# GpSimd drains after every group of four indirect DMAs in a graph network kernel

## The chip, the cores and the metric

The kernel runs on one core of one Trainium2 chip. The metric is the device time of one execution in microseconds (us), lower is better. Before the change it is 5252.78 us, the median of 3 runs (5245.05 to 5259.6).

## The reference

The program is a pre-norm graph network on 100,000 nodes with 128 features and 25,000 edges (src, dst). It adds four layers to x, one after the other, each on `h = relu(layernorm(x))`:

```python
x = x + gcn(h)      # sum over edges of w * h[dst] into src, plus h/degree
x = x + sage2(h)    # two SAGE convolutions: mean over edges of h[src] into dst, two matmuls each
x = x + mlp(h)      # message MLP on [h[src], h[dst], edge_attr], mean into dst, update MLP, layernorm
x = x + mean(h)     # mean over edges of h[dst] into src, two matmuls, relu
```

Each layer reads rows of nodes by the edges' indices and sums messages by the edges' other end. Nodes with no edge need only the parts without neighbours ("dense" work).

## The kernel before

All edges are padded to 50 chunks of 512 (P = 128 partitions, T = 4 tiles), worked on as 10 rounds (RD) of 5 streams (G); chunk `i * G + c` is round i of stream c. Six stages follow the setup: gcn, sage1, sage2, mlp, mean and final. Each stage is one block of five engine programs, and ends with a drain and a barrier on every engine (the block's end, and lines 854 and 855). The first five also carry the dense work of all 100,000 rows as further streams, whose steps stand in the same queues on TensorE, VectorE, ScalarE and SyncE.

GpSimd (POOL) issues only indirect DMAs in the stages, one for each tile of 128 edges, so four for a chunk and purpose:
- **Gathers** (`gather`, L567, recorded as L569): a row of a table in HBM for each of 128 indices, into one tile of SBUF. Each stage has a local `pair(n, i, c)` that issues two of them (L1241 gcn, L1394 sage1, L1542 sage2, L1727 mlp, L1985 mean, L2134 final). A chunk has pairs 0 and 1, in gcn and mlp also 2 and 3 from a second table. A pair is a step `fetch0`, `fetch1`, and so on; `fetch0` of the next round waits until the chunk's buffer has been read by another engine.
- **Adds** (`add_pair`, L1139, recorded as L1151): rows of SBUF are added to a table in HBM by the DMA engines. Since two adds to one row must not overlap, the plan makes one chain over all streams: `add_pair` waits until the pair before in the chain has landed (the `wait_ge` on `e.added`). gcn, sage1 and mlp have steps `add0` and `add1` of two DMAs; sage2 and mean have one step `add` of four.
- **Row writes** (`write_chunk`, L2057, recorded as L2061): in final, four indirect DMAs write a chunk's rows to the output, once for the dst side (`write_d`) and once for the src side (`write_s`). These have a chain as well.

The setup issues 200 gathers of its own (`gathered`, L569 with the tile `xs`), directly and not by `pair`.

The order of the steps on each engine is fixed when the program is built: `Plan` (L278 on) makes a list schedule of all streams' steps with a length for each (FETCH 2600 ns a pair, ADD 3800 ns a pair of adds, 5100 for a row write, LANDED 2800 ns from an add to the next of the chain) and with due times of a table; `rounds` replays this order on every engine. The lengths steer the order only. On the chip each step waits for semaphores: `e.done[c]` counts a stream's steps, `e.gathered[c]` and `e.added[c]` its landed DMAs.

On GpSimd a stage is therefore: the first gathers of all five streams, then the steps in the plan's order, and at its end waits for all adds or writes:

```python
def step(name, i, c):
    if name == "fetch0" and not is_last(i):
        pool.wait_ge(e.done[c], at.after(i, "x1"))
    if name.startswith("fetch") and not is_last(i):
        pair(int(name[5:]), i + 1, c)
    if name in ("add", "add0", "add1"):
        add_pair(pool, e, plan, tb.node, k.leadh, name, i, c, W1)
```

Chunks of a round are consumed a round later than they are fetched: the gathers of round i + 1 are issued in round i, and `keep` (L1176, ScalarE) may overwrite the rows of the adds of round i only when they have landed.

Of the kernel before, what the change touches and what calls it, by code (L numbers as in the profile page):

```python
# [12 lines left out]
T = 4  # L13
# [327 lines left out]
def rounds(step, plan):  # L341

    for name, i, s in plan.order:
        step(name, i, s)
# [32 lines left out]
def is_last(i):  # L377
    return i == RD - 1
# [183 lines left out]
def fill_nodes(steps):  # L562

    return [Node(f"fill{q}", SYNC, 100, after=((step, 0, 0),), main=False) for q, step in enumerate(steps)]

def gather(pool, out, table, idx, signal, offset=0):  # L567

    pool.indirect_dma_start(out, None, table, bass.IndirectOffsetOnAxis(ap=idx, axis=0),  # L569
                            element_offset=offset).then_inc(signal, 16)  # L570
# [568 lines left out]
def add_pair(pool, e, plan, table, leads, name, i, c, offset):  # L1139

    parts = {"add0": range(U), "add1": range(U, T), "add": range(T)}[name]
    pool.wait_ge(e.done[c], e.at.after(i, "keep"))
    held = plan.prior.get((c, name, i))
    if held is not None:
        prior, pair, j = held
        pool.wait_ge(e.added[prior], (j * T + (U if pair == "add0" else T)) * 16)
    for t in parts:  # L1150
        pool.indirect_dma_start(table, bass.IndirectOffsetOnAxis(ap=leads[:, i * G + c, t:t + 1], axis=0), e.comb[c][:, t, :], None,  # L1151
                                element_offset=offset, compute_op=ALU.add).then_inc(e.added[c], 16)

def edge_tail(columns, sum_on, match_after=(), bank=None, whole=False):
# [23 lines left out]
def gcn_phase(nc, k, tb, inp, out):  # L1179

    with ExitStack() as ctx:
# [53 lines left out]
        @block.gpsimd  # L1236
        def _(pool):
            for c in L:
                nc.gpsimd.memset(e.comb[c][:, :, :], 0.0).then_inc(blank, 1)

            def pair(n, i, c):  # L1241
                for t in (2 * n % T, 2 * n % T + 1):
                    at_dst = k.gidx[:, i * G + c, T + t:T + t + 1]
                    if n < 2:
                        gather(pool, x[c][:, t, :], inp["x"], at_dst, e.gathered[c])
                    else:
                        gather(pool, sm[c][:, t, :], tb.small, at_dst, e.gathered[c])

            def step(name, i, c):
                if c >= G:  # L1250
                    return
                if name == "fetch0" and not is_last(i):
                    pool.wait_ge(e.done[c], at.after(i, "y"))
# [3 lines that stand above are left out]
                    add_pair(pool, e, plan, tb.node, k.leads, name, i, c, 0)  # L1257

            for c in L:
                for n in range(4):  # L1260
                    pair(n, 0, c)
            rounds(step, plan)
            for c in L:
                pool.wait_ge(e.added[c], RD * T * 16)
# [59 lines left out]
def sage1_phase(nc, k, tb, inp, out):  # L1324
# [3 lines left out]
    with ExitStack() as ctx:  # L1328
# [63 lines left out]
        @block.gpsimd  # L1392
        def _(pool):
            def pair(n, i, c):  # L1394
                for t in (2 * n, 2 * n + 1):
                    gather(pool, agg[c][:, t, :], tb.node, k.gidx[:, i * G + c, t:t + 1], e.gathered[c])

            def step(name, i, c):
                if c >= G:
                    return  # L1400
# [7 lines that stand above are left out]
            for c in L:  # L1408
                for n in range(2):
                    pair(n, 0, c)  # L1410
            rounds(step, plan)
            for c in L:
                pool.wait_ge(e.added[c], RD * T * 16)
# [70 lines left out]
def sage2_phase(nc, k, tb, inp, out):  # L1484

    with ExitStack() as ctx:
# [52 lines left out]
        @block.gpsimd  # L1540
        def _(pool):
            def pair(n, i, c):  # L1542
                for t in (2 * n, 2 * n + 1):
                    gather(pool, a[c][:, t, :], tb.node, k.gidx[:, i * G + c, t:t + 1], e.gathered[c], W1)

            def step(name, i, c):
                if c >= G:
                    return
                if name == "fetch0" and not is_last(i):
                    pool.wait_ge(e.done[c], at.after(i, "mix"))  # L1550
# [3 lines that stand above are left out]
                    add_pair(pool, e, plan, tb.node, k.leadd, name, i, c, W2)  # L1554

            for c in L:
                for n in range(2):
                    pair(n, 0, c)
            rounds(step, plan)
            for c in L:  # L1560
                pool.wait_ge(e.added[c], RD * T * 16)
# [60 lines left out]
def mlp_phase(nc, k, tb, inp, out):  # L1622
# [3 lines left out]
    with ExitStack() as ctx:  # L1626
# [98 lines left out]
        @block.gpsimd  # L1725
        def _(pool):
            def pair(n, i, c):  # L1727
                for t in (2 * n % T, 2 * n % T + 1):
                    if n < 2:
                        gather(pool, a2[c][:, t, :], tb.node, k.gidx[:, i * G + c, t:t + 1], e.gathered[c], W2)  # L1730
                    else:
                        gather(pool, w[c][:, t, :], tb.node, k.gidx[:, i * G + c, T + t:T + t + 1], gathered2[c])

            def step(name, i, c):
                if c >= G:
                    return
                if name == "fetch0" and not is_last(i):
                    pool.wait_ge(e.done[c], at.after(i, "plus_d"))
# [3 lines that stand above are left out]
                    add_pair(pool, e, plan, tb.sums, k.leadh, name, i, c, 0)  # L1742

            for c in L:
                for n in range(4):
                    pair(n, 0, c)
            rounds(step, plan)
            for c in L:
                pool.wait_ge(e.added[c], RD * T * 16)
# [174 lines left out]
def mean_phase(nc, k, tb, inp, out):  # L1924
# [3 lines left out]
    with ExitStack() as ctx:  # L1928
# [54 lines left out]
        @block.gpsimd  # L1983
        def _(pool):
            def pair(n, i, c):  # L1985
                for t in (2 * n, 2 * n + 1):
                    gather(pool, s3[c][:, t, :], tb.sums, k.gidx[:, i * G + c, T + t:T + t + 1], e.gathered[c])

            def step(name, i, c):
                if c >= G:  # L1990
                    return
                if name == "fetch0" and not is_last(i):
                    pool.wait_ge(e.done[c], at.after(i, "mix_u"))
# [3 lines that stand above are left out]
                    add_pair(pool, e, plan, tb.sums, k.leads, name, i, c, D)  # L1997

            for c in L:
                for n in range(2):  # L2000
                    pair(n, 0, c)
            rounds(step, plan)
            for c in L:
                pool.wait_ge(e.added[c], RD * T * 16)
# [52 lines left out]
def write_chunk(pool, table, rows, idx, signal):  # L2057

    for t in range(T):  # L2060
        pool.indirect_dma_start(table, bass.IndirectOffsetOnAxis(ap=idx[:, t:t + 1], axis=0), rows[:, t, :], None,  # L2061
                                bounds_check=N - 1, oob_is_err=False).then_inc(signal, 16)

class FinalSide:
# [11 lines left out]
def final_phase(nc, k, tb, out):  # L2077
# [4 lines left out]
    with ExitStack() as ctx:  # L2082
# [50 lines left out]
        def _(pool):  # L2133
            def pair(n, i, c):  # L2134
                for t in (2 * n, 2 * n + 1):
                    gather(pool, s34[c][i % 2][:, t, :], tb.sums, k.gidx[:, i * G + c, t:t + 1], e.gathered[c][i % 2])

            def write(name, rows, idx, i, c):
                held = plan.prior.get((c, name, i))
                if held is not None:  # L2140
                    prior, _, j = held
                    pool.wait_ge(written[name][prior], (j + 1) * T * 16)
                write_chunk(pool, out, rows, idx, written[name][c])
# [13 lines left out]
            for c in L:  # L2157
                for n in range(2):
                    pair(n, 0, c)
# [99 lines left out]
```

## Time and profile before

| | |
|---|---|
| Time of the runs | 5252.78 us, median of 3 |
| The profiled execution, first to last instruction | 6243.6 us |
| Mean granted TensorE clock | 0.836 |
| Busy: PE, PEld | 68%, 53% |
| Busy: DVE, ACT | 66%, 59% |
| Busy: POOL | 61% |
| Indirect DMAs issued by POOL | 3200: 200 in the setup, 3000 in the stages |
| DMA engines: hardware queues, POOL's queue | 32.9% and 22.7% of 16 engines |
| Chain that ended last, traced part | mostly "another core or an unknown queue" (6%) in the last stage |

The profiled execution is one execution with the hardware profiler on. Its span is 990.8 us longer than the median of the runs; the page gives no time of it other than the span.
### The profile page before, as it was taken

The numbers are of one execution on the slowest core, as the hardware profiler recorded it, in microseconds if no ns is written. First come the engines' busy times: TensorE is split into PE (matmuls) and PEld (weight loads), VectorE is DVE, ScalarE is ACT, GpSimd is POOL, SyncE is SP. The second block draws the span as 40 slices with busy tenths as digits, with TensorE's granted clock in tenths as the row PEclk, the third lists the DMA queues.
The fourth block names the chain that finished last, engine by engine and source line by source line (L and its number), as shares of the span: only waits on it lengthen the run. The fifth ranks groups of instructions, "written<-read, shape, count | busy, mean of one in ns | idle before, by whom it ended". The sixth has DMA issues, their size and how long they took to land. (4 is left out here: it accounts for less than half of the span.)

```text
span 6243.6 us, 88780 instructions
## 1 busy us (share of the span) xinstructions
PE 4227.3 (68%) x25124; PEld 3337.9 (53%) x25124; DVE 4147.6 (66%) x20553; ACT 3656.1 (59%) x9152; POOL 3838.7 (61%) x3228
## 2 busy tenths in 40 slices
PE   1173777777566766998958888886888846545444
PEld 1052555556455555777736666664666634434333
DVE  1094777778699995776747777785999945434334
ACT  0003767767577774776746677774877845434333
POOL 6605666675577765776747677765777654544554
PEclk7596888888788887999979999998999967667666
DMA  9903656666466664666658788884555531211221
GB/s 251 311 2 112 181 154 172 167 166 169 115 153 151 148 144 113 146 144 132 130 147 220 209 225 216 225 204 113 136 132 128 122 77 58 76 53 63 66 65 36
DMA packets 891523, 878.84 MB, mean 141 GB/s; under 512 B 131106, under 2 KB 671660, under 8 KB 890962
## 3 DMA queue, kind: packets, MB, share of 16 engines
q1 hardware_dynamic: 546568, 575.48, 29.0%
q0 software_dynamic: 224000, 235.91, 22.7%
q10 hardware_dynamic: 120460, 61.78, 3.7%
q8 instruction: 198, 3.24, 0.2%
q14 instruction: 297, 2.43, 0.1%
HBM read 345.70 MB, written 533.16 MB: 141 GB/s over the span
## 5 line engine op out<-in xcount | busy, mean ns | idle before, releaser
L2061 POOL DMA_INDIRECT out<-final_y,leads x200 | 202.2, 1011 | 434.8 <-DVE final_y L2188 328.8
L1151 POOL DMA_INDIRECT node<-gcn_comb,leads x200 | 325.2, 1626 | 193.0 <-ACT gcn_comb L1176 92.5
L1151 POOL DMA_INDIRECT sums<-mean_comb,leads x200 | 327.6, 1638 | 154.1 <-ACT mean_comb L1176 84.4
L1151 POOL DMA_INDIRECT node<-sage_comb,leadh x200 | 329.4, 1647 | 142.4 <-DMA node<-sage_comb,leadh 60.8
L444 PE MATMUL final_p<-wT,final_hT 128*128 128x128 f32 x800 | 223.0, 393 | 274.9 <-remote 141.4
L1151 POOL DMA_INDIRECT sums<-mlp_same,leadh x200 | 325.7, 1628 | 131.4 <-issue 54.2
L1151 POOL DMA_INDIRECT node<-sage_comb,leadd x200 | 319.5, 1597 | 140.7 <-issue 54.2
L839 PE MATMUL hist<-lo,hi 128*126 128x400 f16 x800 | 162.1, 361 | 261.4 <-issue 136.3
L444 PEld LDWEIGHTS final_p<-wT,final_hT 128*128 128x128 f32 x800 | 170.8, 264 | 305.1 <-remote 144.9
L569 POOL DMA_INDIRECT mlp_a<-node,gidx x200 | 207.2, 1036 | 197.2 <-DVE mlp_v L1778 128.6
L785 DVE TENSOR_SCALAR hi<-iota,parts 128x252 f16<-128x252 f16 x400 | 146.0, 378 | 245.7 <-remote 159.0
L569 POOL DMA_INDIRECT gcn_x<-in_x,gidx x200 | 198.1, 991 | 168.8 <-DVE gcn_y L1283 107.1
L444 PE MATMUL gcn_p<-wT,gcn_dhT 128*128 128x128 f32 x1056 | 228.9, 346 | 76.6 <-ACT gcn_dhT L986 40.0
L839 PEld LDWEIGHTS hist<-lo,hi 128*126 128x126 f16 x800 | 114.2, 148 | 309.6 <-DVE lo L786 140.8
L569 POOL DMA_INDIRECT sage_agg<-node,gidx x200 | 203.6, 1018 | 110.4 <-issue 49.4
L437 PE MATMUL final_p<-ident,final_h 128*128 128x128 f32 x600 | 120.3, 339 | 213.5 <-ACT final_h L431 141.7
L444 PEld LDWEIGHTS gcn_p<-wT,gcn_dhT 128*128 128x128 f32 x1056 | 194.0, 228 | 117.3 <-ACT gcn_dhT L986 50.2
L569 POOL DMA_INDIRECT mean_s<-sums,gidx x200 | 202.5, 1013 | 83.7 <-issue 57.3
L437 PE MATMUL sage_p<-ident,sage_dh 128*128 128x128 f32 x840 | 150.0, 310 | 151.4 <-ACT sage_dh L431 109.3
L569 POOL DMA_INDIRECT sage_a<-node,gidx x200 | 200.3, 1001 | 80.8 <-issue 57.5
L569 POOL DMA_INDIRECT xs<-in_x,gidx x200 | 194.8, 974 | 86.9 <-issue 62.2
L431 ACT ACTIVATE sage_dh<-sage_dx,sage_dn_shift,sage_dn_rstd 128x128 f32<-128x128 f32 x560 | 228.5, 482 | 32.8 <-DVE sage_dn_shift L420 14.9
(367 smaller groups left out, 17207.2 us busy)
## 6 DMA issues: line engine op xcount, KB each, us to landing
node<-b SPq DMA_DIRECT2D x400, 256.0 KB
sums<-zero_row SPq DMA_DIRECT2D x400, 256.0 KB
node<-zero_row ACTq DMA_DIRECT2D x50, 1152.0 KB
sage_dx<-in_x SPq DMA_DIRECT2D x70, 256.0 KB
out<-sage_dy SPq DMA_DIRECT2D x70, 256.0 KB
gcn_dx<-in_x SPq DMA_DIRECT2D x66, 256.0 KB
out<-gcn_dy SPq DMA_DIRECT2D x66, 256.0 KB
x_src<-xs SPq DMA_DIRECT2D x50, 256.0 KB
```

What stands on the lines that cost most here:

```text
L431: tiles(lambda t: nc.scalar.activation(out[:, t, :], x[:, t, :], func, bias=b.sh[:, t:t + 1], scale=b.rs[:, t:t + 1])).then_inc(done, 1)
L437: return tiles(lambda t: nc.tensor.transpose(ps[:, t * P:(t + 1) * P], x[:, t, :], ident))
L444: last = nc.tensor.matmul(o, xT[:, t * P:(t + 1) * P], w, start=True, stop=plus is None and bias is None)
L569: pool.indirect_dma_start(out, None, table, bass.IndirectOffsetOnAxis(ap=idx, axis=0), element_offset=offset).then_inc(signal, 16)
L785: nc.vector.tensor_scalar(hi[c][:, n * T + t, :], iota[:, 0:2 * HIGH], part[:, 0:1], None, ALU.is_equal)
L839: last = nc.tensor.matmul(hist[0:HIGH, n, b, 0:LOW], hi[c][:, n * T + t, b * HIGH:(b + 1) * HIGH], lo[c][:, n * T + t, :], start=False, st ...
L1151: pool.indirect_dma_start(table, bass.IndirectOffsetOnAxis(ap=leads[:, i * G + c, t:t + 1], axis=0), e.comb[c][:, t, :], None, element_off ...
L2061: pool.indirect_dma_start(table, bass.IndirectOffsetOnAxis(ap=idx[:, t:t + 1], axis=0), rows[:, t, :], None, bounds_check=N - 1, oob_is_er ...
```

## The change

A new function `settle` issues one drain on GpSimd. It is called behind the fourth gather of each group of four (pair 1, and in gcn and mlp also pair 3), behind the fourth add of a chunk, and behind the fourth row write of a chunk. The setup's gathers are left as they are. The plan and its lengths are not changed, and neither is any wait.

```diff
+def settle(pool):
+
+    pool.drain()
+
+
 def gather(pool, out, table, idx, signal, offset=0):
...
     for t in parts:
         pool.indirect_dma_start(table, bass.IndirectOffsetOnAxis(ap=leads[:, i * G + c, t:t + 1], axis=0), e.comb[c][:, t, :], None,
                                 element_offset=offset, compute_op=ALU.add).then_inc(e.added[c], 16)
+        if t == T - 1:
+            settle(pool)
...
                     else:
                         gather(pool, sm[c][:, t, :], tb.small, at_dst, e.gathered[c])
+                if n % 2 == 1:
+                    settle(pool)
...
             def pair(n, i, c):
                 for t in (2 * n, 2 * n + 1):
                     gather(pool, agg[c][:, t, :], tb.node, k.gidx[:, i * G + c, t:t + 1], e.gathered[c])
+                if n % 2 == 1:
+                    settle(pool)
...
     for t in range(T):
         pool.indirect_dma_start(table, bass.IndirectOffsetOnAxis(ap=idx[:, t:t + 1], axis=0), rows[:, t, :], None,
                                 bounds_check=N - 1, oob_is_err=False).then_inc(signal, 16)
+        if t == T - 1:
+            settle(pool)
```

The `pair` functions of sage2, mlp, mean and final get the same two lines as that of sage1.

## Rows read from the trace of the kernel before

**Rows 1.** Windows by stage: us; busy us (count) of PE, PEld, DVE, ACT, POOL.
```profile
476.00:1645.00 1169.00, 818.72 (x4960) 646.12 (x4960) 839.37 (x4522) 784.34 (x2000) 725.86 (x605) 0.83 0.59 156
1645.00:2430.00 785.00, 499.23 (x2800) 388.17 (x2800) 691.28 (x3850) 556.15 (x1450) 532.97 (x400) 0.83 0.61 140
2430.00:3172.00 742.00, 640.63 (x4280) 543.19 (x4280) 503.62 (x2190) 503.45 (x1200) 519.71 (x400) 0.95 0.62 135
3172.00:4296.00 1124.00, 916.59 (x5510) 701.97 (x5510) 793.37 (x3630) 754.12 (x1850) 734.25 (x600) 0.91 0.77 203
4296.00:5068.00 772.00, 617.53 (x3660) 489.93 (x3660) 659.50 (x3180) 579.48 (x1450) 530.15 (x400) 0.92 0.54 123
5068.00:6244.00 1176.00, 569.41 (x3100) 452.00 (x3100) 469.76 (x2350) 476.36 (x1200) 592.59 (x600) 0.69 0.21 63
```

**Rows 2.** Waits of POOL for other engines: us in total, times, longest; and one issue gap.
```profile
POOL out L2061 <- DVE final_y L2188: 328.8, 27, 35.3
...
POOL mlp_a L569 <- DVE mlp_v L1778: 128.6, 22, 32.3
...
POOL gcn_x L569 <- DVE gcn_y L1283: 107.1, 14, 14.7
POOL node L1151 <- ACT gcn_comb L1176: 92.5, 11, 18.1
POOL sums L1151 <- ACT mean_comb L1176: 84.4, 14, 12.0
POOL node L1151 <- ACT sage_comb L1176: 75.9, 18, 9.2
...
POOL gcn_sm L569 <- issue: 60.6, 199, 0.3
...
POOL sage_agg L569 <- DVE sage_x L1434: 49.2, 33, 6.3
```

**Rows 3.** The same view: waits of POOL for an add's landing.
```profile
POOL node L1151 <- DMA node<-sage_comb,leadh: 60.8, 28, 4.1
...
POOL sums L1151 <- DMA sums<-mlp_same,leadh: 44.3, 15, 4.3
...
POOL node L1151 <- DMA node<-gcn_comb,leads: 37.7, 13, 4.1
...
POOL node L1151 <- DMA node<-sage_comb,leadd: 23.3, 8, 3.9
...
POOL sums L1151 <- DMA sums<-mean_comb,leads: 10.7, 4, 3.3
```

**Rows 4.** Timeline of POOL in sage1: start us, us, what, idle time before.
```profile
2311.43 2.07 POOL L1151 DMA_INDIRECT node<-sage_comb,leadh  x1 [0.31 <-issue]
2315.99 1.73 POOL L1151 DMA_INDIRECT node<-sage_comb,leadh  x1 [2.49 <-DMA node<-sage_comb,leadh]
```

**Rows 5.** Drains on POOL by line: ns min/median/max, first and last start us.
```profile
L576 POOLq DRAIN  x1: 26153/26153/26153, 280.6 to 280.6; - x1
...
L1182 POOLq DRAIN  x1: 6830/6830/6830, 1637.2 to 1637.2; - x1
...
L2082 POOLq DRAIN  x1: 9032/9032/9032, 6233.7 to 6233.7; - x1
...
L854 POOLq DRAIN  x6: 107/119/157, 1644.3 to 6242.9; - x6
...
L855 POOLq DRAIN  x6: 46/46/46, 1644.8 to 6243.3; - x6
```

**Rows 6.** Timeline of POOL: the last indirect DMAs of the setup, gcn and final.
```profile
289.62 1.09 POOL L569 DMA_INDIRECT xs<-in_x,gidx  x1 [0.30 <-issue]
...
1633.65 1.54 POOL L1151 DMA_INDIRECT node<-gcn_comb,leads  x1 [0.30 <-issue]
...
6231.33 0.97 POOL L2061 DMA_INDIRECT out<-final_y,leads  x1 [0.30 <-issue]
```

**Rows 7.** Busy tenths of the DMA engines, 290 to 310 us in 40 slices.
```profile
DMA  9999814999659925999999999620000000000000
```

More of the change, by code:

```diff
@@ L1544, in pair @@
                     gather(pool, a[c][:, t, :], tb.node, k.gidx[:, i * G + c, t:t + 1], e.gathered[c], W1)
+                if n % 2 == 1:
+                    settle(pool)
             def step(name, i, c):
@@ L1732, in pair @@
                         gather(pool, w[c][:, t, :], tb.node, k.gidx[:, i * G + c, T + t:T + t + 1], gathered2[c])
+                if n % 2 == 1:
+                    settle(pool)
             def step(name, i, c):
@@ L1987, in pair @@
                     gather(pool, s3[c][:, t, :], tb.sums, k.gidx[:, i * G + c, T + t:T + t + 1], e.gathered[c])
+                if n % 2 == 1:
+                    settle(pool)
             def step(name, i, c):
@@ L2062, in write_chunk @@
                                 bounds_check=N - 1, oob_is_err=False).then_inc(signal, 16)
+        if t == T - 1:
+            settle(pool)
 class FinalSide:
@@ L2136, in pair @@
                     gather(pool, s34[c][i % 2][:, t, :], tb.sums, k.gidx[:, i * G + c, t:t + 1], e.gathered[c][i % 2])
+                if n % 2 == 1:
+                    settle(pool)
             def write(name, rows, idx, i, c):
```

## The prediction

> **What bounds the kernel now.** I read the windows by stage first, because a mean over the span hides stages with different limits. In none of the six stages is an engine busy throughout [rows 1]: POOL has 726 of 1169 us in gcn, 533 of 785 in sage1, 520 of 742 in sage2, 734 of 1124 in mlp, 530 of 772 in mean, 593 of 1176 in final. But busy time is not all that POOL's queue costs. Next come the waits of POOL: each indirect DMA starts 0.30 us after the end of the one before even where nothing holds it (60.6 us over 199) [rows 2]. With 600, 400, 400, 600, 400 and 600 DMAs that is 180 or 120 us a stage. POOL's own work is then 906, 653, 640, 914, 650 and 773 us, which is 78, 83, 86, 81, 84 and 66% of the stages. So in the first five stages POOL is as near to a bound as the busiest other engine (DVE 88% in sage1, PE 86% in sage2 and 82% in mlp), and in final it waits for others.
>
> What POOL waits for otherwise is short. The six largest of its waits for VectorE and ScalarE in the first five stages come to 538 us (128.6 + 107.1 + 92.5 + 84.4 + 75.9 + 49.2), and final's largest to 329 us [rows 2]. Its waits for an add to land are few, 68 over 400 steps of adds, 177 us in all [rows 3]. The reason is in the plan: a pair of gathers usually stands between two pairs of adds, so that the landing passes behind other descriptor work. That cover is what the change touches.
>
> **What a drain waits for.** The change removes nothing and moves nothing. It adds 750 drains: 150 in gcn (two groups of gathers and one of adds for each of 50 chunks), 100 in sage1, 100 in sage2, 150 in mlp, 100 in mean, 150 in final (one of gathers, two of row writes). No stage of the kernel before has a drain within its work, but each has some at its end, and the setup has one directly behind its gathers. That one began at 280.6 us, while gathers were still queued in front of it, and lasted 26.15 us, to 306.8 us [rows 5]. The last gather ended on POOL at 290.7 us [rows 6], and the DMA engines went quiet in the 27th half-microsecond after 290, at about 303.5 us [rows 7]. So this drain did not end with the descriptors, but after the data. I take it that a drain on POOL ends only when all indirect DMAs before it have landed.
>
> The Trainium skill (Perfetto Trace Analysis, Per-engine timelines) puts DRAIN under the instructions that the sequencer handles alone, with no other actor than the semaphores. By that rule 750 drains would cost what L855's do, 46 ns each, some 35 us; the 26.15 us drain disagrees with it.
>
> **Price of one drain.** It has three terms.
> First, the landing and the restart. They have rows where an add waits for the pair before: idle 2.49 us in place of 0.30 [rows 4], and on average 37.7/13 = 2.90 us in gcn, 60.8/28 = 2.17 in sage1, 23.3/8 = 2.91 in sage2, 44.3/15 = 2.95 in mlp, 10.7/4 = 2.68 in mean [rows 3]. I use them for gathers too, whose landing has no row of its own. From each goes the 0.30 us gap that was there anyway. For final's row writes the nearest row is its end: the last write ended at 6232.3 us [rows 6] and the drain behind its landing wait began at 6233.7 [rows 5], 1.4 us. The restart adds 0.5: in gcn the same stretch was 2.0 us (1635.2 to 1637.2), where a wait up to the next add is 2.50.
> Second, the drain's own time once all has landed. The ends are far apart: 0.05 to 0.16 us for a drain shortly after another, and 6.8 and 9.0 us for the ones at the ends of gcn and final, which began when everything had landed already [rows 5]. In between lies what has been issued since the last drain: nothing in the one case, some 600 DMAs in the other. Per DMA that is 6.83/600 = 0.011 us; the setup's drain gives at most (306.8 - 290.7)/200 = 0.08. Four DMAs are far nearer to none than to 200, so I take 0.12 plus a share for four, between 0.17 and 0.44: 0.26 us.
> Third, what is queued behind. Every later gather and add of all streams is held, and the pair of gathers that used to hide the landing of an add cannot do so across a drain. The other engines wait for these DMAs a round later, so a single drain harms nobody; the sum on POOL does.
> That makes 2.86, 2.13, 2.87, 2.91, 2.64 and (1.4 + 0.5 - 0.3 + 0.26) 1.86 us a drain.
>
> **The sum**, stage by stage, is POOL's work plus its drains against the stage's present length:
> gcn 906 + 150 x 2.86 = 1335, 166 over 1169. sage1 653 + 213 = 866, 81 over. sage2 640 + 287 = 927, 185 over. mlp 914 + 437 = 1351, 227 over. mean 650 + 264 = 914, 142 over. Together 801 us, if POOL never waited for another engine. It will: at a stage's start and end, and where the fixed order is unlucky. I keep 30% of the 538 us, 161 us; the rest is slack that drains fill. In final 773 + 279 = 1052 us is still below 1176, so it isn't bound by POOL; but its chains go through POOL's queue, and I let half of the 279 us show, 140 us. The setup is unchanged. Sum: 801 + 161 + 140 = 1102 us on a span of 6243.6 us, 17.7%.
> The median of the runs, 5252.8 us, is 990.8 us below that span. Scaled with it, the new time is 6180 us; if the landing, which isn't the engines' work, keeps its length, it is 5253 + 1102 = 6355. I take the middle, **6270 us**.
> The bounds: with no slack filled at all, all drains show, 1630 + 279 = 1909 us, which is 6860 to 7160 us. With all slack filled and drains of 2.0 us in place of 2.7, 801 falls to some 370 us to which a part of the slack is added: about 5700 us.
>
> **Rivals.**
> The fixed price. The 6.8 to 9.0 us of the late drains are paid by each drain that has any DMA before it. For it: the setup's (200 DMAs) and gcn's and final's (600) are not in proportion to their number. Against it: a second drain costs 0.12 us. Then POOL would carry 4536 us of stage work plus 750 x 9 us, 11,300 us, and the time is 9500 to 12,000 us. Chance 0.07.
> The cheap drain. It waits only until the descriptors are made, and costs 0.12 us and a cold restart, 0.2 to 0.4 us in all, 150 to 300 us on POOL, a good third of them visible: 5300 to 5400 us. For it: the short drains of L854 and L855. Against: the setup's. This is near what the skill's rule above says. Chance 0.05.
> The other side, not slower. The drain is the sequencer's alone, which reads ahead: the setup's began 9 us before the last gather did. If it holds only the sequencer, for 46 ns, then it is over before the queued DMAs are and POOL sees no gap; 35 us spread over 750 places vanish, also if the builder drops drains as empty. It decides for a drain that ends before the last DMA in front of it does. The time would be 5253 us. The only such drain of the trace ended 16 us after it. Chance 0.04, with 0.01 of it for a gain by DMAs that collide less.
> The forecast has 0.84.
>
> **Chances and range.** 0.3%, 16 us, is about what a measurement of this kernel can tell from no change. The range reaches from 5700 to 7100 us: the forecast's two bounds. It leaves out the rivals, 0.16. Faster 0.01, same 0.03, slower 0.96.
>
> **What the profile after would show.** 750 more DRAIN rows on POOL at `settle`'s line, with a median of 2 to 4 us each, as they start while DMAs before them still run. Idle time of POOL before the first DMA of each group of 2 to 3 us instead of 0.30. The 2.5 us waits for adds should mostly vanish, as a drain has taken them over. POOL's waits for VectorE and ScalarE should shrink in the first five stages, and waits of VectorE and TensorE for DMAs should grow. The drains at the stages' ends should fall from 6 to 9 us to well below 1 us; if they don't, the second term is wrong. All stages should be longer, mlp by most. I am wrong if drains have a median under 0.5 us, or over 6 us, or if the stages grow by the full 1909 us, which would mean that slack fills nothing.

## The result and the profile after

The changed kernel takes 7015.3 us, the median of 4 runs (7009.0 to 7029.18), against 5250.07 us for the kernel before (4 runs, 5245.05 to 5259.6). The ratio is 1.3357, interval 1.3327 to 1.3387: slower by 1765 us. The forecast was 6270 us. The direction and the range held; the size was too small by 745 us.

The page of the changed kernel begins:

```profile
span 7027.4 us, 89530 instructions
PE 4295.2 (61%) x25124; PEld 3406.3 (48%) x25124; DVE 4128.4 (59%) x20553; ACT 3649.4 (52%) x9152; POOL 3866.6 (55%) x3228
```

The span agrees with the runs here. For the profile of before it did not (6243.6 against 5253 us), so the first experiment took a new profile of the unedited kernel, on a chip where it runs in 5265 us (`ctrl`, below). Its page begins:

```profile
span 5246.6 us, 88780 instructions
PE 4000.3 (76%) x25124; PEld 3169.2 (60%) x25124; DVE 4131.0 (79%) x20553; ACT 3632.5 (69%) x9152; POOL 3860.8 (74%) x3228
```

It is the code of [rows 1] with the same count of instructions and, within 2%, the same busy time of DVE, ACT and POOL, in a span 997 us shorter. Against this profile the change has to be read. The windows by stage of the changed kernel (us; busy us of PE, PEld, DVE, ACT, POOL; clock, DMA share, GB/s):

```profile
338.00:1669.00 1331.00, 820.03 (x4960) 654.58 (x4960) 829.25 (x4520) 783.02 (x2000) 730.07 (x605) 0.81 0.51 137
1669.00:2631.00 962.00, 544.12 (x2800) 426.33 (x2800) 689.53 (x3850) 555.25 (x1450) 531.04 (x400) 0.74 0.50 114
2631.00:3546.00 915.00, 654.20 (x4280) 558.89 (x4280) 501.58 (x2190) 502.24 (x1200) 515.21 (x400) 0.85 0.50 110
3546.00:4973.00 1427.00, 910.54 (x5510) 702.32 (x5510) 786.23 (x3630) 746.63 (x1850) 721.40 (x600) 0.81 0.61 160
4973.00:5908.00 935.00, 656.66 (x3660) 517.20 (x3660) 658.83 (x3180) 579.52 (x1450) 529.49 (x400) 0.84 0.44 102
5908.00:7027.00 1119.00, 558.85 (x3100) 438.86 (x3100) 467.40 (x2350) 480.61 (x1200) 596.06 (x600) 0.70 0.22 66
```

and of the unedited kernel in `ctrl`:

```profile
321.00:1300.00 979.00, 752.87 (x4960) 597.08 (x4960) 828.78 (x4520) 777.94 (x2000) 734.25 (x605) 0.90 0.69 186
1300.00:2056.00 756.00, 488.39 (x2800) 380.26 (x2800) 688.86 (x3850) 554.88 (x1450) 535.62 (x400) 0.85 0.64 145
2056.00:2745.00 689.00, 622.32 (x4280) 530.32 (x4280) 500.83 (x2190) 500.26 (x1200) 519.93 (x400) 0.97 0.66 146
2745.00:3736.00 991.00, 883.22 (x5510) 678.91 (x5510) 787.18 (x3630) 743.87 (x1850) 727.90 (x600) 0.95 0.85 230
3736.00:4450.00 714.00, 595.73 (x3660) 472.09 (x3660) 655.53 (x3180) 578.28 (x1450) 533.94 (x400) 0.95 0.58 133
4450.00:5247.00 797.00, 506.38 (x3100) 402.08 (x3100) 469.22 (x2350) 475.12 (x1200) 600.35 (x600) 0.80 0.31 93
```

No engine does more in its stage than before, except that TensorE's matmuls are longer where its clock is lower (0.79 of full speed over the run): it idles between chunks. All six stages grew: by 352, 207, 225, 436, 222 and 323 us, together 1764 before rounding. The setup adds 17 us (338 in place of 321); `gathers` and `spaced` below have the same 17 us, `adds` and `twice` do not, and the setup has none of the new drains, so it isn't they, and it stays unexplained.

In `ctrl`, DMA instructions, memsets and the 0.30 us between them fill POOL for 914, 656, 640, 908, 654 and 780 us, 4552 of the 4925 us of the stages, 92%; in final 98%. That is the prediction's "POOL's own work", as it had it (906, 653, 640, 914, 650, 773), in stages that are 4 to 32% shorter than those of [rows 1].

Now the drains. By line, on POOL (ns min/median/max, first and last start), with those at the ends of gcn and final, which were 6.8 and 9.0 us [rows 5]. The source lines of this kernel are some lines further on than before (L1151 is now L1156, for example):

```profile
L569 POOLq DRAIN  x750: 3405/5973/13829, 340.1 to 7021.4; - x188
...
L1189 POOLq DRAIN  x1: 147/147/147, 1668.1 to 1668.1; - x1
...
L2101 POOLq DRAIN  x1: 53/53/53, 7026.5 to 7026.5; - x1
```

A row of 6 us doesn't mean that a drain costs 6 us: it starts when the sequencer reaches it, with DMAs of the group still before it on the engine. What it costs is seen from POOL's timeline, here in sage1 (start, us, what, idle before):

```profile
2104.02 1.02 POOL L574 DMA_INDIRECT sage_agg<-node,gidx  x1 [0.30 <-issue]
2105.35 0.98 POOL L574 DMA_INDIRECT sage_agg<-node,gidx  x1 [0.31 <-issue]
2108.97 1.62 POOL L1156 DMA_INDIRECT node<-sage_comb,leadh  x1 [2.65 <-issue]
2110.90 1.68 POOL L1156 DMA_INDIRECT node<-sage_comb,leadh  x1 [0.30 <-issue]
...
2115.67 1.02 POOL L574 DMA_INDIRECT sage_agg<-node,gidx  x1 [3.10 <-issue]
```

Behind the fourth gather POOL is idle 2.65 us, behind the fourth add 3.10 us, where the gap would otherwise be 0.30. The trace also has the time at which the DMA engines moved the last packet of each group. With it, the mean over the drains splits into 1.70 us from the last DMA's end on POOL to the landing (0.85 to 0.97 for row writes, 3.3 for mlp's gathers from `node`), 0.57 us from the landing to the drain's end, and 0.78 us to the next DMA: 3.05 in place of 0.30 us, so **2.75 us a drain**. The shortest time from the landing to a drain's end is 0.39 us, and no packet of POOL's queue lands between the end of a drain and the next DMA. 750 of them are 2063 us in POOL's queue. 4552 + 2063 = 6615 us, and the stages take 6689. POOL's queue is now all but the whole time.

POOL's waits agree (us in total, times, longest). "Issue" now holds most of the drains. The wait for `final_y` that was the largest of before [rows 2] is gone. The waits for adds to land [rows 3] seem to be all still there:

```profile
POOL node L1156 <- issue: 409.4, 513, 5.8
POOL sums L1156 <- issue: 307.3, 345, 7.9
POOL out L2078 <- issue: 297.0, 383, 5.0
POOL mlp_w L574 <- issue: 248.7, 200, 6.4
...
POOL node L1156 <- DMA node<-sage_comb,leadh: 55.5, 19, 4.0
POOL node L1156 <- DMA node<-gcn_comb,leads: 53.1, 18, 3.5
POOL node L1156 <- DMA node<-sage_comb,leadd: 41.4, 13, 4.5
POOL sums L1156 <- DMA sums<-mlp_same,leadh: 34.7, 13, 3.6
...
POOL sums L1156 <- DMA sums<-mean_comb,leads: 19.3, 7, 3.0
```

That is 204 us in 70 waits, against 213 in 87 in `ctrl`. But the timeline has a drain in 41 of the 70: there the view puts the drain's time down to the landing, which comes shortly before the drain's end. Only 29, 81 us, are waits at which no drain stood. They are all in gcn, sage1 and mlp, where a chunk's adds are two pairs and no drain stands between them, and 28 of them come directly behind another add. In sage2 and mean, where the four adds are one step, none is left. Waits of POOL over 0.5 us without a drain come to 102 us in 37 places in all.

### The profile page after: what moved, and what is told of

It reads as the page before. It is cut to its first block and busy times, and to the rows that moved or that the text cites. A ratio compares the mean times of both kernels' runs of the same rounds, so it can differ in the third digit from the quotient of the medians.

```text
span 7027.4 us, 89530 instructions
## 1 busy us (share of the span) xinstructions
PE 4295.2 (61%) x25124; PEld 3406.3 (48%) x25124; DVE 4128.4 (59%) x20553; ACT 3649.4 (52%) x9152; POOL 3866.6 (55%) x3228
## 5 line engine op out<-in xcount | busy, mean ns | idle before, releaser
L1156 POOL DMA_INDIRECT sums<-mlp_same,leadh x200 | 324.6, 1623 | 272.2 <-issue 149.9
L1156 POOL DMA_INDIRECT node<-sage_comb,leadh x200 | 327.5, 1638 | 236.9 <-issue 131.3
L1156 POOL DMA_INDIRECT node<-gcn_comb,leads x200 | 322.5, 1612 | 226.1 <-issue 143.3
L1156 POOL DMA_INDIRECT sums<-mean_comb,leads x200 | 325.6, 1628 | 205.4 <-issue 157.3
L1156 POOL DMA_INDIRECT node<-sage_comb,leadd x200 | 317.1, 1586 | 191.0 <-issue 134.7
L476 PE MATMUL mlp_p<-mlp_same,mlp_v 128*128 128x256 f32 x400 | 122.7, 460 | 390.8 <-DVE mlp_same L1089 390.7
L574 POOL DMA_INDIRECT mlp_w<-node,gidx x200 | 197.2, 986 | 248.7 <-issue 248.7
L1089 DVE TENSOR_SCALAR mlp_same<-mlp_krow,rec 128x256 f32<-128x256 f32 x200 | 69.8, 412 | 405.2 <-DMA sums<-mlp_same,leadh 404.1
L574 POOL DMA_INDIRECT gcn_sm<-small,gidx x200 | 198.8, 994 | 196.4 <-issue 196.4
L437 PE MATMUL gcn_p<-ident,gcn_dh 128*128 128x128 f32 x792 | 140.7, 309 | 264.9 <-ACT gcn_dh L431 264.3
L574 POOL DMA_INDIRECT final_s<-sums,gidx x200 | 198.0, 990 | 183.4 <-issue 169.8
L431 ACT ACTIVATE mlp_dh<-mlp_dx,mlp_dn_shift,mlp_dn_rstd 128x128 f32<-128x128 f32 x240 | 98.5, 483 | 381.1 <-DVE mlp_dn_shift L420 380.4
L476 PEld LDWEIGHTS mlp_p<-mlp_same,mlp_v 128*128 128x128 f32 x400 | 87.3, 230 | 411.3 <-DVE mlp_same L1089 396.9
L2078 POOL DMA_INDIRECT out<-final_od,final_rows_d x200 | 199.1, 995 | 158.3 <-issue 147.5
L574 POOL DMA_INDIRECT xs<-in_x,gidx x200 | 234.8, 1174 | 85.7 <-issue 60.7
```

What stands on the lines that cost most here:

```text
L431: tiles(lambda t: nc.scalar.activation(out[:, t, :], x[:, t, :], func, bias=b.sh[:, t:t + 1], scale=b.rs[:, t:t + 1])).then_inc(done, 1)
L437: return tiles(lambda t: nc.tensor.transpose(ps[:, t * P:(t + 1) * P], x[:, t, :], ident))
L476: last = nc.tensor.matmul(ps[:, h * HALF:(h + 1) * HALF], msg[:, b, :], same[:, block, :], start=(n == 0), stop=(n == len(terms) - 1))
L1089: last = nc.vector.tensor_scalar(e.same[c][:, t, :], key_half(e, c, t), field(k, i, c, key)[:, t:t + 1], weight[:, t:t + 1], ALU.is_equal, ...
```

## The experiments

None of them leaves out or changes a part of the computation. Ratios are to the kernel before on the same chip. The question was where the missing 745 us were: in the price of a drain (theory A: each is dearer than 2.55 us), or in the slack (theory B: the price is nearly right, but far less of it is hidden). The rival to both was that the drain isn't a wait for landing at all but a fixed cost.

### On a chip where the kernel before takes 5265 us

**ctrl**: the kernel before, unedited.

> The kernel before, not edited. The profile of before spans 6243.6 us where its runs took 5250; the profile of the changed kernel spans 7027 where its runs took 7015. Theory: that one profiled execution of before was held up by the recording (its setup ended at 486 us with VectorE stalls of 40 us, that of the changed kernel some 150 us sooner), and a second profile of the same kernel spans 5250 us within 1%. Rival: the profiler always adds some 990 us to this kernel, and the second profile spans 6200 us or more; then the 1765 us of the runs and the 784 us between the two profiles disagree for a reason that lies in the change.

Measured 5247.41 us, ratio 0.9984 (0.996 to 1.0008), and the profile above. Its span is 997 us below that of the profile the prediction read, for the same code. So a profile doesn't add the 991 us. Nor was it a recording that held up one execution, as was expected: on three other chips (below) the kernel before takes 6103 to 6226 us, the medians of 8 to 19 runs. The difference is a property of the chip or of its state. The lower clock of TensorE (0.836 in place of 0.901) doesn't explain it: TensorE is busy 227 us more in the first profile, not 997.

**gathers**: drains behind gathers only, 400 of them.

```diff
-        if t == T - 1:
-            settle(pool)
```

(in `add_pair` and in `write_chunk`)

> Drains behind the groups of gathers alone, 400 of 750. Theory (every drain holds GpSimd's queue until the four DMAs before it have landed, 2.75 us more than the 0.30 us gap, and what slack the stages have is filled first): 400 x 2.8 = 1120 us on the queue, 250 of it hidden in slack, 6050 to 6200 us. Rival (the drains behind adds carry the cost, since these hold the chain of adds, and gathers are fetched a round ahead and can land whenever they like): under 5600 us.

Measured 6362.19 us, 1.2112 (1.1991 to 1.2233): +1097 us over the 5264.83 of before, or 2.74 us a drain. More than expected.

**adds**: the other 350, behind adds and row writes.

```diff
-                if n % 2 == 1:
-                    settle(pool)
```

(in all six `pair` functions)

> Drains behind adds and row writes alone, 350 of 750. Theory (queue time is queue time): 250 x 2.7 + 150 x 2.1, with the group of adds often followed by a wait for their landing anyway: 5750 to 6000 us, and the two halves together show less than the whole, as each fills the same slack. Rival (the chain of adds carries the cost): 6500 us or more, nearly the whole loss.

Measured 6003.44 us, 1.1429 (1.1341 to 1.1517): +739 us, 2.11 us a drain, just above the expected band (whose sum counts 150 row-write drains where there are 100). Added up the two halves cost 1836 us, together 1765. If each alone had hidden much in slack that both share, the whole would cost more than the two added, as was expected; it doesn't, so hardly any slack of that kind was left on this chip, which speaks for B. A reason for costing less may lie in the line found by `spaced` below: all 3000 DMAs pay their 0.042 us once in either run alone, 126 us, and also only once together. But the intervals of the two runs, some 60 and 45 us either way, are as large as the difference of 71 us, so this isn't shown.

**waits**: no drain, and in each place a wait for the semaphore of the same four DMAs, as in sage1:

```diff
-                    settle(pool)
+                    pool.wait_ge(e.gathered[c], (i + 1) * T * 16)
```

> No drain; in each drain's place GpSimd waits for the semaphore of the same four DMAs. Theory (a drain is a wait for the landing, plus its own 0.57 us from the last completion packet to its end): a semaphore wait ends some 0.3 us after the packet and the next DMA starts 0.7 us later, so each group saves 0.2 to 0.3 us against the drain; 6780 to 6900 us. Rival (the cost is the drain's own, a flush of the engine and of the queue of instructions read ahead): under 5700 us.

Measured 6662.77 us, 1.2684 (1.2578 to 1.2791), 1398 us over its before and 352 us less than the drains, 0.47 us each. Below the expected band: more of the cost is the drain's own than was expected, but four fifths of it is there with no drain at all, as plain waiting for data. The timeline shows the same picture as with drains, with the landing now named as the releaser:

```profile
1800.77 0.98 POOL L569 DMA_INDIRECT sage_agg<-node,gidx  x1 [0.30 <-issue]
1803.61 1.62 POOL L1151 DMA_INDIRECT node<-sage_comb,leadh  x1 [1.85 <-DMA sage_agg<-node,gidx]
1805.53 1.75 POOL L1151 DMA_INDIRECT node<-sage_comb,leadh  x1 [0.30 <-issue]
1809.74 1.03 POOL L569 DMA_INDIRECT sage_agg<-node,gidx  x1 [2.47 <-DMA node<-sage_comb,leadh]
```

1.85 and 2.47 us in place of the 2.65 and 3.10 of the drains: 0.8 and 0.6 us less. That the drain waits for the landing is thereby shown, not only read from the setup's row.

**twice**: a drain for each pair, 1500 in all.

```diff
-                if n % 2 == 1:
-                    settle(pool)
+                settle(pool)
...
-        if t == T - 1:
+        if t in (U - 1, T - 1):
```

> A drain after every pair of gathers or of adds and after two of four row writes, 1500 drains. Theory (each drain holds the queue for a landing): the 750 further ones cost 2.5 to 2.75 us each, less where a wait for an add stood at that place anyway (some 150 of them), 1500 to 2000 us more, 8500 to 9000 us. Rival (the cost goes by the DMAs that must be cleared, so half as many a drain cost half): near 7015 us.

Measured 8676.2 us, 1.6492 (1.6417 to 1.6568): 1661 us over the changed kernel for 750 more drains, 2.2 us each, a little under the first 750's 2.35. This is what a landing costs again and again; a fixed 7 to 9 us would have added over 5000.

**spaced**: a drain only for every 2nd, 4th, 8th, 16th, 25th or 50th group, by stage, 128 in all.

```diff
+EVERY = {"gcn": 2, "sage1": 4, "sage2": 8, "mlp": 16, "mean": 25, "final": 50}
+STAGE = ["gcn", 0]
+
 def settle(pool):
-    pool.drain()
+    STAGE[1] += 1
+    if STAGE[1] % EVERY[STAGE[0]] == 0:
+        pool.drain()
```

(and each stage's function sets `STAGE` to its name and 0)

> Drains at growing distances: after every 2nd group of four DMAs in gcn, 4th in sage1, 8th in sage2, 16th in mlp, 25th in mean, 50th in final, 128 in all. It measures a drain's own time, from the last landing to its end, against the number of DMAs since the last drain, which was 0.57 us for 4 and 5.7 to 9.0 us for 400 to 600. Theory (the drain goes through a list of DMAs not yet cleared, which has a bound, at 0.03 to 0.08 us each): 0.8 us after 8, 1.0 after 16, 1.9 after 32, 3.5 after 64, and the 6 us reached at 100 to 200. Rival A (a fixed cost that falls due once enough DMAs have passed): a step from 0.6 to 6 us. Rival B (0.01 us for each DMA, no bound): 0.7 after 16, 1.0 after 64, 2.5 after 200. Whole time: 5250 plus 128 x 2.5 = 320 us and the rising own time, 5450 to 5650 us.

Measured 5603.88 us, 1.0649 (1.0605 to 1.0693): 343 us for 128 drains, 2.68 each. The run was for the drain's own time, which the prediction could not place between 4 and 200 DMAs. POOL's timeline has the idle time behind drains that close 8, 32, 64, 100 and 200 DMAs (gcn, sage2, mlp, mean, final; the rows of mlp and final close 66 and 202):

```profile
354.13 0.94 POOL L580 DMA_INDIRECT gcn_x<-in_x,gidx  x1 [3.11 <-issue]
...
2363.06 0.94 POOL L580 DMA_INDIRECT sage_a<-node,gidx  x1 [3.67 <-DVE sage_hT L1595]
...
3258.96 0.94 POOL L580 DMA_INDIRECT mlp_w<-node,gidx  x1 [6.16 <-issue]
...
4404.97 1.62 POOL L1162 DMA_INDIRECT sums<-mean_comb,leads  x1 [7.22 <-DVE mean_n_rstd L417]
...
5062.89 1.01 POOL L2089 DMA_INDIRECT out<-final_y,leads  x1 [9.47 <-issue]
```

The medians over the drains of a stage are 3.05 (8 DMAs), 3.29 (16), 4.15 (32), 6.38 (64), 7.2 (100) and 9.6 us (200). The part from landing to the drain's end, worked out from the packets of this run, of `twice`, `gathers`, `adds` and of the changed kernel, is 0.46 us with 2 DMAs since the last drain, 0.55 with 4, 0.71 with 8, 0.88 with 12, 1.04 with 16, 1.70 with 32, 3.15 with 64, 4.9 with 100. That is a line of about 0.38 + 0.042 us per DMA, close to the theory (0.8 after 8, 1.0 after 16, 1.9 after 32, 3.5 after 64). There is no step, as rival A had it, and the slope is four times rival B's. Up to 16 DMAs the same count gives the same time in runs that have it in different stages, so the stage isn't what counts. It doesn't go on: 198 to 202 DMAs give 4.5 us in the setup and 7.1 to 8.2 in final, both in this run, and the rows of the drains behind 400 to 600 are 5.7 to 9.0 us long.

The line is that of a drain that stands directly behind its DMAs and has begun before they land. A drain that begins only when all have landed costs twice as much for each. The ends of the stages in `gathers` and `spaced` show it, where POOL waits for all adds and then drains; these four rows close 16 DMAs (`spaced`) and 20, 38 and 40 (`gathers`):

```profile
L1507 POOLq DRAIN  x1: 1351/1351/1351, 3043.4 to 3043.4; - x1
...
L1496 POOLq DRAIN  x1: 1677/1677/1677, 3276.7 to 3276.7; - x1
...
L1187 POOLq DRAIN  x1: 3150/3150/3150, 1561.1 to 1561.1; - x1
...
L1941 POOLq DRAIN  x1: 3311/3311/3311, 5434.6 to 5434.6; - x1
```

They lie on 0.04 + 0.082 us per DMA, as do the ends with 28, 30 and 34. So a drain takes something for each DMA issued since the last drain, even when all of them have long landed. That a drain which begins early does half of this while it waits would explain the 0.042; it wasn't tested. At 0.082 us each, the 5.7 to 9.0 us behind 400 to 600 DMAs are worth some 70 to 110 DMAs (an estimate), so the bound lies about there.

### On chips where the kernel before takes 6100 to 6230 us

The next runs fell on other chips, on which the unedited kernel takes 6102.87, 6102.8 and 6226.07 us: the condition of the profile of before. Expectations in absolute times were mostly written for 5250; where the kernel before takes 6100 they can't be met, and the ratios and differences have to be compared.

**empty**: in each drain's place a wait that is always fulfilled.

```diff
-            settle(pool)
+            pool.wait_ge(e.done[c], 1)
```

> In each drain's place GpSimd waits for a count of 1 of the stream's own step semaphore, which is always reached already. The step costs the sequencer an instruction and the engine nothing. Theory (the landing is what costs): within 0.5% of the kernel before, 5230 to 5280 us. Rival (any instruction between two groups breaks the reading ahead, so that the next DMA starts 0.75 us after in place of 0.30): 750 x 0.45 = 340 us, 5500 to 5600 us.

Measured 6121.15 us, 1.0025 (1.001 to 1.004), 18 us. A wait for what is already reached costs next to nothing here. It is a weaker test than was meant: the 750 waits make only 239 further instructions (89019 in place of 88780), since the others are carried by an instruction that was there anyway, a DMA for example. The rival's price of 0.45 us for each would be 108 us for those 239. The 18 us speak against it, though on this chip part of what POOL's queue loses is hidden.

**empty2**: the same kernel again, on a third chip.

> The waits for what is always reached, once more. On the chip where the kernel before takes 6103 us they cost 0.25%, with GpSimd far from its bound. Where the kernel before takes 5250 us GpSimd's queue has 92% of the stages, and a step that broke the reading ahead would show in full. There: theory within 0.5%, 5230 to 5290 us; rival (0.45 us each) 5500 to 5600 us. If the job runs where before takes 6100: 1.0025 again, and the point stays open.

Measured 6260.05 us, 1.0073 (1.0039 to 1.0106), 34 us for 750 places, 0.05 us each, or 0.14 for each further instruction. The ratio is above the 1.0025 that was expected again. The cost where the kernel before takes 5250 us wasn't measured.

**double**: two drains in a row.

```diff
     pool.drain()
+    pool.drain()
```

> Two drains in a row in each place, 1500 in all, 750 of them with nothing to clear. Theory (a drain costs the landing of what is out, a fixed part of some 0.38 us and 0.04 us for each DMA cleared, and a second one finds nothing): 0.05 to 0.15 us each with the step between them, 40 to 150 us more than the changed kernel, 7050 to 7160 us. Rival (each drain has a fixed cost of 0.4 us or empties the engine anew for 0.75 us): 7300 to 7600 us.

Measured 7251.6 us, 1.1879 (1.1832 to 1.1926). Against `after2` below, from another chip with the same time of before, the second drains cost 104 us, 0.14 each. That is within the expected 40 to 150 us. Their rows say that a drain with nothing to wait for is nearly free:

```profile
L569 POOLq DRAIN  x750: 3659/5957/13092, 490.6 to 7258.0; - x188
...
L570 POOLq DRAIN  x750: 41/41/203, 498.0 to 7262.7; - x188
```

**finalonly** and **finalonly2** (one kernel, two chips): drains in the last stage alone, 150 of them.

```diff
-                if n % 2 == 1:
-                    settle(pool)
```

(in the other five `pair` functions, and the two lines in `add_pair`)

> Drains in the last stage alone, 150 of 750. In the prediction half of final's drain time was to be hidden, since POOL seemed 66% taken there; in the clean profile of the kernel before it is 98% taken (782 of 797 us). Theory now: nothing is hidden, the stage grows by 320 to 340 us as in the changed kernel, 5570 to 5600 us, and the other stages keep their length. Rival (the prediction's): 140 us, 5390 us.

> Drains in the last stage alone once more. On the chip where the kernel before takes 6103 us they cost nothing (0.996), its last stage being 1157 us long there with 774 of GpSimd's work. If this job runs where the kernel before takes 5250 and final 797 us: theory 5570 to 5600 us, nothing hidden; rival 5390 us, half of it hidden. If it runs where before takes 6100: 0.995 to 1.0 times before again.

Measured 6078.7 us, 0.9958 (0.9938 to 0.9978), and 6079.13 us, 0.9955 (0.9937 to 0.9973). On such chips the last stage takes 1125 and 1122 us with 150 drains, and 1157 to 1176 without a drain (the profile of before, `empty` and `empty2`); on the others 797 without and 1119 with. The drains fit entirely into time that POOL spent waiting, and on the slow chips the stage is even 32 us shorter than in `empty` on the same chip. What became of that waiting is told at the end of this section.

**after2**: the changed kernel.

> The changed kernel, not edited. The kernel before took 5250 to 5265 us in the first measurements and 6103 us on another chip, where VectorE got a count of TensorE in the setup some 40 us late. If this job runs where the kernel before takes 6100: theory (drains fill what time GpSimd has left, and there it has 850 us more to give) 7050 to 7150 us, 1.16 to 1.17 times before, in place of 1.336. Rival (the cost of a drain adds up whatever else waits): 6103 + 1765 = 7870 us. If it runs where the kernel before takes 5250: 7015 us again.

Measured 7147.89 us, 1.1715 (1.1692 to 1.1739), +1045 us, as the theory had it. Its windows of gcn and final:

```profile
486.00:1812.00 1326.00, 827.34 (x4960) 659.52 (x4960) 830.09 (x4520) 783.25 (x2000) 729.95 (x605) 0.80 0.51 137
...
6026.00:7148.00 1122.00, 565.40 (x3100) 443.57 (x3100) 468.42 (x2350) 480.06 (x1200) 596.84 (x600) 0.70 0.22 66
```

Beside the changed kernel's on the first chip (1331 and 1119) little differs but the setup, 486 in place of 338 us. The kernel before is 838 to 853 us slower on such a chip, the changed one 133 us. What makes these chips slow therefore costs almost nothing in the stages once the drains are there.

Where the time goes can be seen in the waits of the first profile. The largest are for "remote", a count on a semaphore that arrives with no instruction of the trace ending just before it (us in total, times, longest):

```profile
ACT final_hT L1899 <- remote: 217.9, 22, 25.2
DVE hi L785 <- remote: 159.0, 5, 41.8
PEld final_p L444 <- remote: 144.9, 13, 25.0
PE final_p L444 <- remote: 141.4, 13, 24.8
```

All of its "remote" waits come to 1902 us in 421 cases, on all engines together (where PE and PEld, or two engines behind one another, wait at the same time, it is counted twice); 939 us of them are in final. `ctrl` has none. `after2` has 173 us in 44 cases, and the largest three are in the setup:

```profile
DVE hi L790 <- remote: 111.9, 3, 41.8
```

The setup shows one of them closely. TensorE finished a row of 16 matmuls of L839 and then had nothing to do; in the first profile (PE, then DVE):

```profile
66.36 5.45 PE L839 MATMUL hist<-lo,hi 128*126 128x400 f16 x16 [10.02 <-issue]
107.44 2.93 PE L839 MATMUL hist<-lo,hi 128*126 128x400 f16 x8 [35.63 <-DVE lo L786]
```

```profile
103.87 0.29 DVE L785 TENSOR_SCALAR hi<-iota,parts 128x252 f16<-128x252 f16 x1 [37.56 <-remote]
```

TensorE is done at 71.8 us; the count on which VectorE waits for its buffers, due from a matmul that ended at 56.34, is recorded at 103.84; VectorE goes on at 103.87, and TensorE behind it. In `ctrl` the same matmuls follow each other 0.6 us apart. The setup of the first profile has five such waits of up to 41.8 us. They come while the DMA engines are filled with the setup's transfers (338 to 340 GB/s), but in `ctrl` these are filled as well (328 to 334 GB/s) and no count is late.

In final the drains do more than fit into the gaps. On the same chip `empty` has 960 us of "remote" waits there in 134 cases, `finalonly` 7 us in 4. The trace has the time of every count, so the late ones can be counted even where nobody waits for them. In final 531 of 2100 counts of VectorE, ScalarE and TensorE come more than 1 us after the end of their instruction in the first profile, 205 with the drains of `finalonly`, 1 in `ctrl`. So with the drains fewer counts are late, and the late ones hardly hold anybody. What delays the counts on some chips, and why it is fewer behind drains, isn't shown by any run here.

## Why the prediction was right in its direction and wrong in its size

- **What a drain waits for**: right. In each of the 750 places the drain ends 0.39 us or more after the last packet, `waits` has most of the cost with no drain at all, the ends of the stages' drains fell from 6.8 and 9.0 us to 0.15 and 0.05 us, `twice` adds a landing a pair. The fixed price falls by `twice`, the cheap drain and the sequencer alone by the result itself, and by the 2.65 and 3.10 us of idle time behind the groups. The Trainium skill (Perfetto Trace Analysis, Per-engine timelines) names no length for a drain; the 46 ns that the prediction put beside its rule hold only for a drain with nothing before it, as `double`'s 41 ns shows. That nothing but the sequencer and the semaphores takes part, as the rule has it, the trace doesn't bear out for GpSimd: the drain's end follows the last packet of its DMAs, and POOL is idle 3.05 us in the mean. One reading was loose: [rows 7] has the DMA engines of all queues, quiet at 303.5 us. POOL's own packets were all moved by 298.3 us, so the setup's drain took 8.5 us beyond its data, and 4.5 us in `ctrl`.
- **The price**: 2.75 us measured where the working averaged 2.55. The own time was 0.57 in place of 0.26: its slope, 0.042 us per DMA, was inside the bounds (0.011 to 0.08, the upper one being that of a late drain), but the base, taken as the 0.12 of a drain without DMAs before it, is 0.38 as soon as there is one. The restart was 0.78 in place of 0.5. The landing was shorter than what was left of the 2.49 to 2.95 us waits. These make 0.2 us a drain, 150 us in all.
- **The slack, which is the step that failed.** The sum was made in stages of 742 to 1176 us [rows 1], and then carried over to runs 991 us shorter, by a scale or by addition. Both keep slack in proportion. But the 991 us were slack: the runs have stages of 689 to 992 us with the same work of POOL. With `ctrl`'s windows the prediction's own terms give 4552 + 1909 = 6461 us for the stages, 1536 over 4925; with 2.75 us a drain 6615, 1690 over, of the 1764 measured. The remaining 74 us are about what POOL still waits where no drain stands, 102 us. For the chip of its profile the sum came near: 1102 us, 17.7%, forecast, and 1045 us, 17.15%, measured by `after2`. That is partly luck. Against the windows of `empty`, the first five stages grew by 1049 us in place of 801 + 161 = 962, and final, which was to grow by 140, became 35 us shorter.
- **Half of final's 279 us hidden**: on the slow chips all of it is (`finalonly`), on the others, where POOL's work filled 98% of the stage, hardly any; final grew by 323 us.
- **The range** held by its upper end. It was to be the forecast's two bounds, but these are 5700 and 7160 us, and it stops at 7100. The case behind the upper bound, in which no slack is filled, is near to what happened: drains dearer by 150 us, and 300 us of them hidden.
- **It would be wrong if the stages grew by the full 1909 us**: they grew by 1764 of the 2063 us that drains took, so some 300 us are hidden, of it about 40 at the ends of the stages, where a drain of 5.7 to 9.0 us had been anyway.
- **Signs**: idle time of 2 to 3 us behind a group, yes. A median drain row of 2 to 4 us, no: it was 5.97 us, hardly below the 6 us that were to mean that the prediction is wrong. The length of the row says little, since it counts DMAs of the group that were still in front. The waits for adds should mostly vanish: yes, from 213 us in 87 waits (`ctrl`) to 81 us in 29, those inside a chunk's two pairs of adds, where no drain stands. POOL's waits for VectorE and ScalarE shrank, as forecast: 7 us are left where no drain stands. Waits of VectorE and TensorE for DMAs grew, as forecast: VectorE's from 355 us (`ctrl`) to 1496, TensorE's from 126 to 502. mlp grew most, yes.

What stays open: what sets the two kinds of chips apart, and why drains make late counts fewer; the 17 us of the setup; what bounds a drain's own time; and the cost of an empty wait on a chip of the 5250 us kind, where the 98% of final would show it.

## What to carry to other kernels

Compare the profile's span with the runs before using any idle time from it. If they differ by a fifth, the profile is of another condition, and its slack may not exist in the runs; work the sum once with the slack and once with POOL's (or any queue's) work alone, and let the second be a case, not the edge of the range. A drain on GpSimd directly behind indirect DMAs costs their landing, 0.4 + 0.04 us per DMA (2 to 100 of them), and 0.8 us up to the next DMA; one that begins when all have landed takes 0.08 us per DMA; where only some data must have landed, a wait on its semaphore is about 0.5 us cheaper, and cheaper still when placed behind other DMAs, as the kernel before has it.

## What the runs showed of the hardware that was not expected

- A drain's own time grows with the DMAs issued since the last one, landed or not. From the landing to its end: 0.55 us for 4, 1.70 for 32, 3.15 for 64, 4.9 for 100. Begun when all have landed: 1.35 us for 16, 3.31 for 40, 5.7 to 9.0 for 400 to 600.
- The same kernel takes 5250 to 5265 us on some chips and 6103 to 6226 on others. On the latter, counts of TensorE, VectorE and ScalarE are recorded late, in final 531 of 2100 by over 1 us, and one of TensorE's in the setup by 47.5 us (56.34 to 103.84 us). A kernel held by POOL's queue differs by 2%, 7015 against 7148 us.
